# Paged attention: a batch's own keys and values loaded ahead of its pages, with the queries and an output store between the pages

## The reference

```
q = x Wq (32 heads of 128);  k, v = x Wk, x Wv (8 heads of 128); RMS norm and rotary embedding of q and k
kc, vc = k_cache[block_table], v_cache[block_table]    # 16 pages of 32 positions per batch: 512 cached keys
k_all, v_all = concat([kc, k]), concat([vc, v])        # 544 keys: the cached ones, then the batch's own 32
scores = q . k_all / sqrt(128), cached keys at or over cache_seqlens masked
x = x + softmax(scores) . v_all Wo
```

## Time and profile before

| | before |
|---|---|
| median of 3 runs (all) | 2220.04 us (2217.65, 2220.04, 2234.28) |
| profiled execution | 2221.79 us, its span 2220.0 us |
| TensorE matmul busy | 2152.6 us, 97% of the span |
| TensorE weight load busy | 1647.3 us, 74% |
| VectorE, ScalarE, GpSimd busy | 1462.8 us (66%), 1392.3 us (63%), 220.3 us (10%) |
| chain that ended last | PE 94%, issue 2%, SP queue 2%, DMA 1% |
| DMA, mean over the span | 490 MB, 221 GB/s |
| DMA share in attention (640 to 1640 us) | 0.95 at 323 GB/s |
| DMA share in the projection (50 to 480 us) | 0.50 at 114 GB/s |
| DMA share in the last stage (1750 to 2220 us) | 0.31 at 94 GB/s |

### The profile page before, as it was taken

The page is one execution under the profiler, slowest core; times in us unless marked ns, Lnnn a source line. Parts: engine busy times, 40 slices in busy tenths (PEclk is TensorE's granted clock), DMA queues, the critical chain, the costliest instruction groups (busy, mean ns, idle before and its releaser), DMA issues.

```text
span 2220.0 us, 77529 instructions
## 1 busy us (share of the span) xinstructions
PE 2152.6 (97%) x30576; PEld 1647.3 (74%) x30576; DVE 1462.8 (66%) x3642; ACT 1392.3 (63%) x4174; POOL 220.3 (10%) x208
## 2 busy tenths in 40 slices
PE   8999999999999999999999999999999999999998
PEld 6888888887666766667676676676777888888886
DVE  5799999994566766667676666666764433433433
ACT  4888888884677777777777777777773222222221
POOL 5211111110000111100000000000003101101101
PEclk9999999999999999999999999999999999999999
DMA  5455545548999999999999999999984333333331
GB/s 193 104 131 113 115 110 117 132 97 272 359 338 319 324 330 317 312 321 329 334 323 319 323 309 328 314 316 308 335 295 145 107 90 101 107 95 101 98 101 50
DMA packets 355010, 490.22 MB, mean 221 GB/s; under 512 B 58994, under 2 KB 191346, under 8 KB 351987
## 3 DMA queue, kind: packets, MB, share of 16 engines
q1 hardware_dynamic: 354674, 485.62, 68.3%
HBM read 397.37 MB, written 88.08 MB: 219 GB/s over the span
## 4 chain that ended last, share of the span: by engine, by line
PE 94%; issue 2%; SPq 2%; DMA 1%; DVE 1%; ACT 1%; ACTq 0%; DVEq 0%
PE o_bank L971 25%; PE s_bank L951 23%; PE acc L730 8%; PE acc L731 8%; PE acc L732 8%; PE proj L1408 5%; PE proj L1410 5%; PE proj L1409 5%; PE wide L1455 1%; PE wide L1450 1%; PE slim L1439 1%; PE wide L1451 1%; PE turn L1429 1%; PE slim L1437 1%; DMA kv<-k_spill 0%
## 5 line engine op out<-in xcount | busy, mean ns | idle before, releaser
L971 PEld LDWEIGHTS o_bank<-p_t,kv 32*128 32x128 f32 x17408 | 519.5, 187 | 134.0 <-issue 132.8
L898 DVE CUSTOM_DVE_ANT_0 probs<-s_bank,mask 128x544 f32<-128x544 f32 x512 | 370.7, 725 | 356.3 <-PE s_bank L951 356.3
L971 PE MATMUL o_bank<-p_t,kv 32*128 32x128 f32 x17408 | 574.8, 277 | 23.5 <-issue 22.7
L951 PE MATMUL s_bank<-kv,q_t 128*32 128x288 f32 (+1 forms) x8192 | 531.3, 397 | 22.7 <-issue 20.6
L856 ACT ACTIVATE probs<-probs,neg_max 128x544 f32<-128x544 f32 x512 | 383.4, 752 | 258.5 <-DVE neg_max L898 246.7
L951 PEld LDWEIGHTS s_bank<-kv,q_t 128*32 128x32 f32 x8192 | 247.7, 110 | 217.1 <-issue 32.4
L912 DVE STREAM_TRANSPOSE p_t<-probs 128x544 f32<-128x544 f32 x512 | 365.3, 731 | 0.4 <-ACT probs L862 0.4
L862 ACT ACTIVATE probs<-probs,inv_sum 128x544 f32<-128x544 f32 x512 | 356.8, 751 | 0.0
L730 PE MATMUL acc<-w_hi,x_hi 128*128 128x512 f32 x764 | 300.5, 393 | 0.0
L731 PE MATMUL acc<-w_lo,x_hi 128*128 128x512 f32 x764 | 300.1, 393 | 0.0
L732 PE MATMUL acc<-w_hi,x_lo 128*128 128x512 f32 x764 | 298.1, 390 | 0.0
(11 more groups left out here) (137 smaller groups left out, 2466.7 us busy)
## 6 DMA issues: line engine op xcount, KB each, us to landing
kv<-in_kv_pages SPq DMA_DIRECT2D x1024, 256.0 KB, 4.6
q_spill<-stage SPq DMA_DIRECT2D x512, 64.0 KB, 1.8
q_t<-q_spill SPq DMA_DIRECT2D x64, 512.0 KB, 5.8
o_spill<-o_t SPq DMA_DIRECT2D x64, 512.0 KB, 6.6
raw<-o_spill SPq DMA_DIRECT2D x64, 512.0 KB, 3.5
kv<-in_w_qkv SPq DMA_DIRECT2D x11, 1024.0 KB, 5.8
v_spill<-stage SPq DMA_DIRECT2D x8, 1024.0 KB, 7.1
k_spill<-stage SPq DMA_DIRECT2D x128, 64.0 KB, 1.8
```

The lines of the kernel that those rows point to most:

```text
L898: nc.vector.tensor_tensor_reduce(out=probs[:, i], in0=s_run(n), in1=mask[:, b % 2], scale=-SCALE, scalar=3.0e38, op0=ALU.add, op1=ALU.min, ...
L951: last = pe.matmul(s_banks[n % 2][rows, columns].rearrange("p (s t) -> p s t", t=PSIZE), q_t[:, b % 2, g, r * S:(r + 1) * S], kv[:, buf, s ...
L971: last = pe.matmul(o_banks[a][:, hh * ROWS:(hh + 1) * ROWS], kv[rows, buf, c, VALUES + hh * HD:VALUES + (hh + 1) * HD], p_t[rows, m % 2, c ...
```

## The change

`load_pages` gets a function that is called ahead of every pair of pages. For batches from 3 on, SP now waits for the buffer, loads own keys and own values, then the 16 page numbers into registers, and then the pages in eight pairs. Ahead of each pair SP waits for a count of `scored`, `b*8 - 10 + pair*3//4`, that is b*8-10 plus 0, 0, 1, 2, 3, 3, 4, 5. Ahead of pair 3 it loads the queries, ahead of pair 5 it stores the output of batch b-3. Batch 2 keeps its order. The pieces of Wo still come last. Sizes, buffers, semaphores and all work of the other engines stay the same.

```diff
-            def load_pages(sp, b):
+            def load_pages(sp, b, before=lambda pair: None):
 ...
                 for i in range(NPP):
+                    if i % 2 == 0:
+                        before(i // 2)
                     sp.dma_start(kv[:, buf_of(b), i],
 ...
             load_pages(sp, 2)
+            def between(b):
+
+                def before(pair):
+                    sp.wait_ge(scored, b * HK - 10 + pair * 3 // 4)
+                    if pair == 3:
+                        load_queries(sp, b)
+                    if pair == 5:
+                        store(b - BUFS)
+
+                return before
+
             for b in range(2, B):
 ...
                 if b >= BUFS:
                     sp.wait_ge(summed, 4 * (b - BUFS + 1))
-                if b > 2:
-                    load_pages(sp, b)
                 load_own_keys(sp, b)
                 load_own_values(sp, b)
-                sp.wait_ge(scored, (b - 1) * HK)
-                load_queries(sp, b)
+                if b == 2:
+                    sp.wait_ge(scored, (b - 1) * HK)
+                    load_queries(sp, b)
+                else:
+                    load_pages(sp, b, between(b))
                 if b in WO_WITH:
 ...
-                if b >= BUFS:
-                    store(b - BUFS)
```

## The result

The changed kernel takes 2268.41 us (median of 4, 2262.0 to 2274.73) against 2220.73 (the profiled executions are counted in), a ratio of 1.0211, 95% interval 1.0167 to 1.0255. I had said 2252 us, 2208 to 2282, with 0.62 for slower. The direction and the place were right. The forecast of 2252 is 1.4% over 2220; the measured time is 16 us over the forecast and within its range. The profiled run is the fastest of the four, 2262.0 us with a span of 2260.2: 40 us over the profiled run of before, where the medians are 48 us apart.

What follows compares the result with a forecast made beforehand. TensorE was to wait for each batch's last landing: two batches take 12.2 + 0.55 + 22.9 = 35.65 us, 17.8 each, +30 us, plus 2 for scatter, 2254 us profiled; median 2252 us, range 2208 to 2282.

Steps and rivals of the forecast that it cites:

- The loop of two batches: Attention: two batches take at least 12.2 us plus the lag; with other stalls 35.65 us, 17.8 a batch.
- the lag: Attention: time from R to a batch's last landing; forecast 22.9 us (21.6 to 23.8), where 20.4 costs nothing.
- R: Attention: the end of the weighing that frees the buffer for a batch's loads; first page forecast 4.6 us after it.
- The waits at the pairs, the wait ahead of the store: nothing.: SP in attention: counts are reached before SP comes to them, so these waits cost nothing, at most 0.4 us a batch.
- This 2.4 us is the part that hurts: Start of a batch's loads: own keys and values first put the first page at R + 4.6 instead of about R + 2.2.
- 2.8 us: Page loads: time added to the last landing by 1.05 MB of queries and store ahead of it, upper end.
- Scatter only adds; 2 us for it: Attention: the loop takes the larger of two times each batch, so variation adds time; 2 us allowed in all.
- stalls inside batches: TensorE within scores: taken as unchanged by the order of transfers; other stalls 0.74 us a batch, 0.55 within the loop.
- inside: TensorE, batches 6 to 63: time over 16.31 us a batch, less idle ahead of first scores; 43 us before, 54 changed.
- the thresholds: Waits for scores at the pairs: rival that they bind and lateness feeds itself, 0.5 us more a batch, 2280 us; chance 0.04.
- The faster rival: Page loads: the DMA queue keeps up, lag 20.7, query waits go; 2205 us, or 2195 with other stalls halved; chance 0.14.
- D: Theory formed after the first follow-up run: a deep queue of issued transfers also delays TensorE while it works.

Runs made afterwards that it cites:

- e3: Changed kernel without the waits for scores at the pairs, keeping the one the queries need: 2274.1 us, ratio 1.0254 to the kernel before.
- e2: Kernel before with only own keys and values moved ahead of the pages: 2217.5 us, ratio 0.9992.
- e6: Changed kernel with the store moved behind the pages: 2225.8 us, ratio 1.0022 to the kernel before.
- e10: Changed kernel with own keys, own values and the store behind the pages, only the queries between them: 2216.9 us, ratio 0.9978 to the kernel before.
- e1: Changed kernel with own keys and values loaded behind the pages again: 2251.7 us, ratio 1.0139 to the kernel before.
- e8: Changed kernel with the queries behind the pages, the store still among them: 2273.0 us, ratio 1.0230 to the kernel before.
- e11: Changed kernel meant to load registers twice, but the second load isn't in the trace, so the changed kernel again: 2272.0 us, ratio 1.0211 to the kernel before.
- e9: Kernel before with transfers spread over the batch by pair waits, next batch's page numbers loaded ahead of pair 4, pair 7's own wait dropped: 2206.7 us, ratio 0.9929.
- e7: Kernel before, loading only the keys of the pages from batch 3 on, computing on old values: 2187.1 us, ratio 0.9848.
- e4: Kernel before with the register load ahead of the wait for the buffer and the queries behind page 4: 2222.0 us, ratio 1.0003.

## Why the prediction was right, and where it was not

- *What bounds it.* The loop of two batches, 12.2 us and the lag, is what the change hits. Measured: from start(b-2) to R 12.76 us (I had 12.75), lag 22.65 in the mean, 21.3 to 24.7 in single batches (I had 22.9, with ends 21.6 and 23.8 for the mean). From R to the first page 3.9 us, not 4.6, since the register load took 0.97 us and not 1.77; from there to the last landing 18.8, not 18.3. Two errors of opposite sign.
- *The waits at the pairs, the wait ahead of the store: nothing.* Right (e3; in the trace SP waits 5.5 us at the pairs and 6.0 ahead of the store, in all batches together).
- *"This 2.4 us is the part that hurts": wrong.* Own keys first costs nothing alone (e2), 9 us with the queries between the pages (e6 against e10), and 17 us with the store there too (changed against e1). The store among the pages is the larger part: back behind them it gives 43 us (e6) or 35 us (e10 against e1); with it there, the queries' place doesn't matter (e8). So the two parts cost more together than apart, as a lag does that costs only beyond what is free. Whether it is the store's bytes or that it is a store was not tested: no run puts a load of that size there. In the sum both were terms of one lag; I had the sum nearly right and the blame wrong. Half of my "2.8 us" for 1.05 MB, the queries, is repaid, since they were the last to land before; the store's half is new in front of the last landing, and measured 1.5 us there (e6).
- *The sum.* Mean lag and loop give (12.76 + 22.65)/2 = 17.7 us; the pace was 18.02. "Scatter only adds; 2 us for it" was the mis-sized term: 0.32 x 57 = 18 us (26 us in e11's trace). Only 31 of the 57 starts wait for a page, but those wait 1.3 us each; where the last landing is early, nothing is given to the next batch. In the profiled executions the forecast of +32 stands against +41: 16 us more for scatter, 7 less because the mean was 17.7 and not 17.8. The medians' +48 has 7 us more, because the profiled execution is the changed kernel's fastest.
- *Which stalls move.* I took the stalls inside batches as independent of the order. In e1 they rose by 38 us, in e9 they fell by 24. Wrong. The 11 us by which "inside" rose in the changed kernel are no more than two of its traces differ by; about half of them go with the clock (below).
- *The rivals.* The queue didn't keep up (share 0.90, not 0.96), and the thresholds don't bind. The faster rival's time, 2205, was reached only by another order (e9, 2206.7), and by relief inside the batches; the waits at their starts stayed (16 us, 13 before).

**The other stalls.** e7 shows that traffic makes them and e1 against e10 that its order does. What it is that arrives late is inferred. In the trace of before, 27 times inside batches (600 to 1650 us) a matmul starts over 0.55 us after the one ahead of it; all 27 times it starts 2.2 to 2.6 us after a packet of the instruction queue does. In the changed kernel it starts 2.2 to 2.7 us after one in 34 of 37 times, in e1 in 53 of 56. These packets come every 5.5 us on average, so chance would give about one in twelve. In the changed kernel and in e1 the packets ahead of such gaps start when 1.9 to 2.0 MB are issued and not landed, the others at 1.5 MB (means); but before it is 1.7 against 1.6, and the same in e4, where "inside" is 55 and not 43. So the depth of the queue is at most a part of it, and D, which e6 missed too, is not shown. The queue's own row (226 packets in 3.70 MB, 16 KB each):

```profile
q8 instruction: 226, 3.70, 0.7%
```

The Trainium skill, Runtime: NRT & Kernel Launch, section Instruction fetch mechanics, says that instructions come in blocks of 16 KiB through a DMA queue of the sequencer's own, and that this is mostly hidden. The size agrees with the row; if the inference is right, it is not hidden in this kernel at a DMA share of 0.95, where e7 gives back 40 us inside the batches. No run held the instruction queue apart, so the link stays an inference, and why e1 has 27 us more inside than the changed kernel, with as much issued and not landed (1.8 MB against 1.7 in the mean), stays open; that the long waits at batch starts let blocks catch up is only a guess.

## What to carry to other kernels

Where loads can't be issued before one instant and are due at another, sum the time from the first to the last landing, and give what isn't due its place behind what is: a store among the last pages cost 35 to 43 us, the queries among the early ones nothing. A part that costs nothing alone can cost beside another, so try parts both alone and taken out of the whole. Moving the last arrival off the critical place (e4) gave nothing, since stalls inside the batches took it back; spreading the issues over the batch, with waits that really bind, gave 0.4%, and 0.7% with the register load moved into one of these waits and the last one dropped. A threshold that the issuer reaches late is no pacing: check its waits in the trace.

## What the hardware showed that I had not expected

**The clock falls after a long wait.** In stretches of the changed kernel around the wait that ends at 1026.26 us (columns as in the earlier trace rows; the last three are granted clock, DMA share, GB/s):

```profile
1023.00:1026.50 3.50, 0.82 (x28) 0.55 (x24) 0.66 (x2) 1.66 (x4) 0.00 (x0) 1.00 1.05 336
1026.50:1030.00 3.50, 3.50 (x36) 1.59 (x32) 0.88 (x3) 0.84 (x2) 0.00 (x0) 0.53 1.03 351
1030.00:1033.50 3.50, 3.50 (x93) 2.67 (x92) 2.71 (x8) 2.14 (x4) 0.00 (x0) 0.98 0.92 303
```

TensorE had been idle 2.68 us; then the granted clock is 0.53 over the stretch, the lower of its two levels (1.2 GHz) for nearly all of it, and 32 matmuls take 3.44 us instead of 2.04. So this late page cost its wait and 1.4 us more. The changed kernel has five such falls between 600 and 1680 us, at the five longest waits of batch starts (2.7 to 4.2 us), and the first scores behind them take 2.7 to 3.9 us, 6.6 us more together than at 2.04 each; the kernel before has one fall. The shorter waits had none, and not every long one has it: in e9 a wait of 3.0 us was followed by scores at full clock.

**The register load took less.** It took 1.77 us in the median before. In the changed kernel, straight behind the own values, it took 0.97 (here in ns, minimum, median and maximum):

```profile
L125 SPq TENSOR_LOAD <-pages x57: 967/972/990, 643.7 to 1652.6; - x57
```

In e1, where it stands behind the wait as before, it took 0.97 us too, so its place isn't the reason. In e4 it took 1.69 and in e9 0.97; the reason stays open.
